# Expert chunks 0 to 5 taken rank by rank, with one chunk prepared ahead, in a fused attention and mixture-of-experts kernel

## What is computed

```python
w, idx = _gate(xf, gate_w)                 # 1024 tokens, the best 6 of 32 experts
c = zeros((T, E)).at[arange(T)[:, None], idx].add(w)
g = einsum('td,eid->tei', xf, w11)         # E = 32, i = 128, d = 256
u = einsum('td,eid->tei', xf, w33)
y = einsum('tei,te,edi->td', silu(g) * u, c, w22)
shared = silu(xf @ sw1.T) * (xf @ sw3.T) @ sw2.T
return y + shared
```

## Time and profile before

| what | value |
|---|---|
| runs | 410.45, 412.38 and 405.9 us, median 410.45 |
| profiled execution, its own time | 408.52 us |
| its span, first to last instruction | 406.7 us |
| mean granted TensorE clock | 0.849 of full speed |
| busy: PE, DVE, POOL, ACT | 287.6, 257.0, 211.5, 167.7 us |

### The profile page before, as it was taken

How to read it: one execution, slowest core, us unless ns; L and a number is a source line. 1 busy time by engine, 2 the same in 40 slices (tenths; PEclk the granted TensorE clock), 3 DMA queues, 4 the chain that set the end, 5 groups by cost and what they waited for, 6 DMA issues and landing times.

```text
span 406.7 us, 5245 instructions
## 1 busy us (share of the span) xinstructions
PE 287.6 (71%) x1471; PEld 216.1 (53%) x1471; DVE 257.0 (63%) x758; ACT 167.7 (41%) x368; POOL 211.5 (52%) x238
## 2 busy tenths in 40 slices
PE   0899975610699999339899396583579899999600
PEld 0444433310679888026466174462569799998400
DVE  4499998570253533175886878798645566656366
ACT  1500003530255554525636534220266688887400
POOL 2577751037433555410511077767775677778830
PEclk9999997655599999958967778789598999999955
DMA  8556699723376651489989222325469855798598
GB/s 236 163 139 180 178 271 270 222 84 116 124 218 196 187 175 50 147 282 319 305 256 365 78 79 92 106 89 178 146 182 289 250 168 156 240 283 274 176 374 283
DMA packets 66062, 80.56 MB, mean 198 GB/s; under 512 B 7643, under 2 KB 55061, under 8 KB 66035
## 3 DMA queue, kind: packets, MB, share of 16 engines
q1 hardware_dynamic: 56547, 62.45, 52.2%
q0 software_dynamic: 7296, 16.93, 12.2%
q10 hardware_dynamic: 2192, 0.86, 0.8%
HBM read 43.70 MB, written 38.01 MB: 201 GB/s over the span
## 4 chain that ended last, share of the span: by engine, by line
PE 52%; DVE 15%; DMA 11%; POOL 10%; issue 7%; ACT 4%; POOLq 1%; SPq 0%; ACTq 0%; DVEq 0%
PE banks L1817 9%; POOL rows_s L688 7%; PE banks L1664 6%; PE banks L1665 5%; PE banks L1666 5%; DMA y_s<-y_sb,place 4%; PE banks L1784 4%; PE banks L1645 4%; PE banks L1646 3%; PE banks L1647 3%; PE banks L1674 2%; POOL y_s L726 2%; DMA rowbuf<-rows_s 2%; PE banks L1910 2%; DMA pre_own<-y_s 2%
## 5 line engine op out<-in xcount | busy, mean ns | idle before, releaser
L726 POOL DMA_INDIRECT y_s<-y_sb,place x88 | 90.8, 1032 | 47.1 <-ACT y_sb L857 24.1
L688 POOL DMA_INDIRECT rows_s<-staged,slot_i x64 | 64.2, 1003 | 57.2 <-DVE staged L1168 38.9
L1664 PE MATMUL banks<-xT_hi,w_hi 128*128 128x224 f32 (+1 forms) x192 | 63.8, 332 | 8.2 <-DVE w_lo L1421 8.0
L1665 PE MATMUL banks<-xT_lo,w_hi 128*128 128x224 f32 (+1 forms) x192 | 56.5, 294 | 0.0
L1666 PE MATMUL banks<-xT_hi,w_lo 128*128 128x224 f32 (+1 forms) x192 | 56.4, 294 | 0.0
L1664 PEld LDWEIGHTS banks<-xT_hi,w_hi 128*128 128x128 f32 x192 | 38.5, 201 | 13.9 <-DVE w_lo L1421 10.9
L1817 PE MATMUL banks<-down_raw,hid 128*104 128x256 f32 (+1 forms) x176 | 44.0, 381 | 1.6 <-DVE hid L1443 1.4
L1784 PE MATMUL banks<-ident,rowbuf 112*128 112x112 f32 (+1 forms) x176 | 25.3, 275 | 27.2 <-DMA rowbuf<-rows_s 22.7
L765 ACT ACTIVATE h_sb<-x_sb,shift,rstd 128x256 f32<-128x256 f32 x22 | 11.7, 590 | 68.8 <-DVE shift L1027 68.8
L857 ACT ACTIVATE y_sb<-banks,meta 112x256 f32<-112x256 f32 (+1 forms) x88 | 36.3, 471 | 8.0 <-PE banks L1817 7.5
L1665 PEld LDWEIGHTS banks<-xT_lo,w_hi 128*128 128x128 f32 x192 | 38.5, 201 | 0.7
(11 more groups left out here) (241 smaller groups left out, 595.5 us busy)
## 6 DMA issues: line engine op xcount, KB each, us to landing
rows_s<-empty SPq DMA_DIRECT2D x5, 2730.0 KB
up_raw<-in_up SPq DMA_DIRECT2D x38, 256.0 KB, 4.7
rowbuf<-rows_s SPq DMA_DIRECT2D x32, 227.5 KB, 3.4
down_raw<-in_down SPq DMA_DIRECT2D x38, 128.0 KB, 4.6
rows_s<-empty SPq DMA_DIRECT2D x7, 633.8 KB
rowbuf<-rows_s SPq DMA_DIRECT2D x8, 316.9 KB
toep<-filt_s SPq DMA_DIRECT2D x16, 128.0 KB, 3.3
h_sb<-y_s SPq DMA_DIRECT2D x4, 512.0 KB, 5.3
```

The lines of the kernel that those rows point to most:

```text
L688: nc.gpsimd.indirect_dma_start(out=rows_s, out_offset=bass.IndirectOffsetOnAxis(ap=slot_i[:, k, b:b + 1], axis=0), in_=staged[:, b, k % BU ...
L726: nc.gpsimd.indirect_dma_start(out=y_s[n], out_offset=bass.IndirectOffsetOnAxis(ap=place[slot][0:TILE[n], t:t + 1], axis=0), in_=y_sb[slot ...
L1664: nc.tensor.matmul(out, wh, xh, start=start, stop=False)
L1665: nc.tensor.matmul(out, wh, xl, start=False, stop=False)
```

## The change

For chunks 0 to 5 each engine prepares only one chunk ahead (`prepares`: steps 0 to 3 prepare s + 1; step 4 prepares 5 and then 6; step 5 prepares 7). From step 6 on the order is that of before. On PE a step of these is `up(s)`, `down(s-1)`, `turn_rows(s+1)`; step 4 is `up(4)`, `down(3)`, `turn_rows(5)`, `down(4)`, `turn_rows(6)`. On ACT it is silu, `take_y(s-1)`, `high_parts(s+1)`. Before the loop only chunk 0 is prepared. PE's wait for all of `add_shared` moves from ahead of chunk 0's transposes to behind `up(0)`. On DVE chunk 0 is split ahead of `stage_values(10)`, and step 0 (with the split of chunk 1) stands between `add_shared(1)` and `stage_values(11)`. `table_turns` moves behind step 8 and `table_codes` behind step 10. On SP the up weights of chunk 5 and the down weights of chunk 4 are loaded ahead of the wait for the last rank, and no longer behind it. For the first feed-forward block nothing changes.

```diff
-        def run_steps(eng, n, step):
+        def run_steps(eng, n, step, begun=0):
             for i in range(FIXED[n]):
-                for r in range(4):
+                for r in range(0 if i else begun, 4):
                     step(i, r, i == 0, False)
...
+        def by_rank(n, i, r):
+            return n == 1 and isinstance(i, int) and 4 * i + r < TOPK1
+
+        def prepares(i, r):
+            return ((1,), (1,), (1,), (1,), (1, 2), (2,))[4 * i + r]
...
-                    if not (last and r >= 2):
+                    if n == 1 and first and r == 3:
+                        sp.wait_ge(f.w_split, 2)
+                        load(up_raw[1][:], of_unit(up_d, TOPK1 - 1, 0), f.up_in[1])
+                        sp.wait_ge(f.down_done, 1)
+                        load(down_raw[0][:], of_unit(down_d, TOPK1 - 2, 0), f.down_in[0])
+                        sp.wait_ge(f.x_split, 2)
+                        wait_sent(TOPK1 - 1)
+                        load(rowbuf[1][0:TILE[n], 0:TILES[n]], rows_of(TOPK1 - 1), f.rows_in[1])
+                    elif not (last and r >= 2):
...
-                    if not first and not own:
+                    if not first and not own and not (n == 1 and isinstance(i, int) and s == TOPK1 - 2):
...
+                    if by_rank(n, i, r):
+                        if 0 < s < TOPK1 - 1:
+                            take_y(i, r, -1)
+                        high_parts(i, r, prepares(i, r)[0])
+                        if s == TOPK1 - 2:
+                            take_y(i, r, 0)
+                            high_parts(i, r, 2)
+                        return
...
+                    if by_rank(n, i, r):
+                        for ahead in prepares(i, r):
+                            low_parts(i, r, ahead)
+                    elif first:
...
+                    if n == 1 and isinstance(i, int) and s == 8:
+                        table_turns(1, 2)
+                    if n == 1 and isinstance(i, int) and s == 10:
+                        table_codes(1)
...
                     stage_values(9)
                     shared_hid(3)
                     add_shared(0)
-                    table_turns(1, 2)
+                    low_parts(0, 0, 0)
                     stage_values(10)
                     add_shared(1)
+                    step(0, 0, True, False)
                     stage_values(11)
-                    table_codes(1)
-                low_parts(0, 0, 0)
-                low_parts(0, 1, 0)
...
-                    pe.wait_ge(x_added, X_ATT1 + 4)
...
+                    if by_rank(n, i, r):
+                        s = 4 * i + r
+                        up(i, r, first)
+                        if 0 < s < TOPK1 - 1:
+                            down(i, r, -1)
+                        if s == 0:
+                            pe.wait_ge(x_added, X_ATT1 + 4)
+                        turn_later(i, r, prepares(i, r)[0])
+                        if s == TOPK1 - 2:
+                            down(i, r, 0)
+                            turn_later(i, r, 2)
+                        return
```

More of the change, by code:

```diff
@@ L322, in ahead_of @@
             def ahead_of(r, prepare):
[L323 to L327, removed]
-            return ahead_of
+                for t in range(2 * r) if r < 2 else (r,):
+                    prepare(t)
+            return ahead_of
+        def by_rank(n, i, r):
+            return n == 1 and isinstance(i, int) and 4 * i + r < TOPK1
+        def prepares(i, r):
+            return ((1,), (1,), (1,), (1,), (1, 2), (2,))[4 * i + r]
         def is_zero(count):
@@ L862, in _ @@
                 high_parts(0, 0, 0)
-                high_parts(0, 1, 0)
+                if n == 0:
+                    high_parts(0, 1, 0)
                 def step(i, r, first, last):
@@ L871, in step @@
                         .then_inc(f.silu_made, 1)
+                    if by_rank(n, i, r):
[6 more added lines that the diff above has]
+                        return
                     if first:
-                        if r and not (n == 0 and r == 2):
+                        if r and r != 2:
                             take_y(i, r, -1)
@@ L1389, in _ @@
                     route_first()
[L1390 to L1399, removed]
-                    table_turns(1, 2)
-                    stage_values(10)
-                    add_shared(1)
-                    stage_values(11)
-                    table_codes(1)
                 def low_parts(i, r, ahead):
@@ L1444, in step @@
                     ins.then_inc(f.hid_made, 1)
-                    if first:
+                    if by_rank(n, i, r):
+                        for ahead in prepares(i, r):
+                            low_parts(i, r, ahead)
+                    elif first:
                         ahead_of(r, lambda t: low_parts(i, t, 2))
@@ L1448, in step @@
                         low_parts(i, r, 2)
-                turns = run_steps(dve, n, step)
+                    if n == 1 and isinstance(i, int) and s == 8:
+                        table_turns(1, 2)
+                    if n == 1 and isinstance(i, int) and s == 10:
+                        table_codes(1)
+                if n == 0:
+                    low_parts(0, 0, 0)
+                    low_parts(0, 1, 0)
+                else:
+                    stage_values(6)
+                    shared_hid(1)
+                    stage_values(7)
+                    stage_values(8)
+                    shared_hid(2)
+                    table_sums(1, 2)
+                    stage_values(9)
+                    shared_hid(3)
+                    add_shared(0)
+                    low_parts(0, 0, 0)
+                    stage_values(10)
+                    add_shared(1)
+                    step(0, 0, True, False)
+                    stage_values(11)
+                turns = run_steps(dve, n, step, n)
                 last_k = TOPK[n] - 1
@@ L1823, in _, with turn_later @@
                 turn_rows(0, 0, 0)
[L1824 to L1828, removed]
+                def turn_later(i, r, ahead=2):
+                    c, first_unit, _, _, _ = chunk_of(n, i, r, ahead)
                     back = (1, 2)[n]
@@ L1831, in turn_later @@
                         pe.wait_ge(f.x_split, c - back + 1)
-                    turn_rows(i, r, 2)
+                    turn_rows(i, r, ahead)
                 def step(i, r, first, last):
+                    if by_rank(n, i, r):
[10 more added lines that the diff above has]
+                        return
                     if first:
-                        if n == 0 and r == 2:
+                        if r == 2:
                             down(i, r, -1)
```

## The result

The changed kernel takes 414.54 us (median of 4 runs, 412.61 to 416.62), the kernel before 410.49 us (4 runs): ratio 1.0137, 95% interval 1.0086 to 1.0188. The medians lie 4.05 us apart and the ratio says 5.6 us, since it compares the means of the fast runs alone and one run of the kernel before (412.38 us) counts as slow. The time is inside the range of the prediction, but the loss is well beyond the 1.4 us that stood there as the likeliest. The profiled execution took 412.66 us with a span of 410.8 us, 4.1 us more than that of the kernel before.

The account below looks back on a forecast made before the run. Bound: the path to `up(9)` at 321.56 us, through chunk 5's late rows and a slow `y_sb` scatter. `up(9)` 0.5 us later plus 0.9 us for the table, on 408.52, gave 409.9 us; range 404.5 to 415.0.

Parts of the forecast that it names:

- the circle of the steps: Steps one chunk ahead: `up(s)`, `down(s-1)`, transposes and split of s + 1, then `up(s+1)`; 5.02 or 7.15 us by clock.
- The rule that what moves `up(9)` moves the end by as much: Landmark: start of `up(9)`, 321.56 us before; its shift moves the end equally unless a later wait takes it back.
- When step 0 starts: Start of the chunks on PE: `up(0)` at about 282.0, `up(1)` at about 288.0, `stage_values(11)` hidden with 4.6 us to spare.
- What a step costs rank by rank: Steps one chunk ahead: 5.02 us at full clock, 7.15 at half, against ranks coming every 5.04 us.
- Which clock?: PE in the new steps, idle about 2.3 us each: clock goes up and down, mean of 6.09 us a step likeliest.
- The sum, to `up(9)`: `up(4)` at 306.3, chunk 5 turned at 309.4, `up(5)` at 312.4, `up(9)` at 322.1: 0.5 us after 321.56.
- slow rival: Clock lost for all of steps 1 to 4: `up(9)` at 326.3, 5.6 us slower, 414.1 us; chance 18%.
- The table in the loop: `table_turns` and `table_codes` on DVE behind steps 8 and 10: 0.9 us lost, bounds 0 and 4.44.
- The stall of 312 to 321: `place` held by a 7.32 us `y_sb` scatter: already in the landmark, does not come back; landed by 318.8.
- The loads that SP issues ahead of the last rank: 384 KB of early weights: cost at nothing; at best take 1.3 us out of what queues later.
- The rule of the Trainium skill: Matmul bursts parted by long DMA waits begin at half rate; by it alone the sum is 414.1 us.
- The first rival: Clock holds: steps of 5.04 us, sends the floor, `up(9)` at 318.3, 3.3 us gained, 406.1 us; chance 27%.

Follow-up runs that it names:

- e5b: Changed kernel with 9, 5 and 10 small matmuls into an unused bank filling PE's gaps, rerun on another chip: 408.17 us, ratio 0.9980 to the kernel before.
- e3: Kernel before with only `table_turns` and `table_codes` moved behind steps 8 and 10: 409.64 us, ratio 0.9999.
- e6b: Changed kernel with PE's gaps filled as in e5b and the table's pieces put back ahead of the loop: 409.12 us, ratio 0.9987 to the kernel before.
- h2b: h1 without the early loads, the weights of chunk 5 behind its rows again: 411.67 us, ratio 1.0020 to the kernel before.
- h1: Kernel before, two chunks ahead, but chunk 5 prepared only in step 4, with the change's early weight loads: 407.45 us, ratio 0.9939.
- e1: Changed kernel with `table_turns` and `table_codes` put back ahead of the loop: 414.17 us, ratio 1.0114 to the kernel before.

## Why the prediction was right or wrong

The step that failed is the clock's share of the steps, with the tail as a smaller second. The view of how the chunks begin and the circle of the steps held. The rule that what moves `up(9)` moves the end by as much did not: `up(31)` lost 1.2 us more than `up(9)` in the changed kernel, and in e5b it gained 1.6 us less. The places, by the prediction's own steps:

- *When step 0 starts.* Foreseen 282.0 and 288.0 for `up(0)` and `up(1)`; 282.76 and 288.70 came, in a trace that is 0.6 us later from ahead of the chunks. `stage_values(11)` was hidden. The last rank started at 295.25 and not at 294.45, which the prediction names as a sign of being wrong, but POOL waited for nothing (0.30 us between scatters, as ever), and the last scatter started at 299.04 for 298.77.
- *What a step costs rank by rank.* At full clock 5.02 was foreseen and 5.15 came; at half clock 7.15 and 7.32. `down` was priced too low: 0.68 us is its time between transposes and an `up`. Between an `up` and transposes, as in these steps, it took 0.86 us at full clock (304.78 to 305.64) and 1.70 at half (291.40 to 293.10), for 1.36 foreseen; the 3.1 us of the rest, 2.92 measured, hid half of that.
- *Which clock?* This step failed. I took the mean, 6.09 us, as the likeliest. Steps 1 and 2 and the `up` of step 4 ran at half clock, and only step 3 at full. Up to `up(4)` the steps average (308.49 - 288.70) / 3 = 6.60 us; chunk 5 was turned at 312.37 for 309.4, and `up(5)` started at 315.23 for 312.4. Of the 2.5 us that `up(9)` came later than foreseen, 1.5 lie in steps 1 to 3 and 0.8 in `up(4)` and `down(3)`.
- *The sum, to `up(9)`.* Foreseen 322.1 (0.5 late), measured 324.63. The slow rival, with 18% on it, said 326.3; it had the mechanism. That its 414.1 us lie so near the measured 414.54 is partly luck: its `up(9)` was 1.7 us too late, since one step kept the clock, and it had nothing for the tail, in which another 1.2 us was lost from `up(9)` to `up(31)` (4.4 - 3.2). The likeliest sum also stood on the profiled execution's 408.52 us, 2 us under the median of the runs, so that 409.9 us was no loss at all against them.
- *The table in the loop.* 0.9 us foreseen; some 0.4 us in the trace of the changed kernel (2.97 - 2.585), nothing that can be measured in the runs (e3 at 0.9999, e6b no better than e5b).
- *The stall of 312 to 321.* It did not come back, as foreseen: `up(6)` to `up(9)` came 2.5 to 2.6 us apart.
- *The loads that SP issues ahead of the last rank.* Cost at nothing, 1.3 us at best. In the changed kernel they delay chunk 5's rows by about 1.2 us, which nobody waits for. Their worth shows only where `down(4)` stands ahead of chunk 6 and PE has caught up with chunk 5: h2b against h1, 0.8%.
- *The rule of the Trainium skill* ("TensorE: Matmul & The Clock Gate", section "HAM oscillation — how this bites in real kernels") says that matmuls parted by waits that are long enough begin each time at the slow clock; taken for every step, that was the slow rival's case. The trace agrees for three of the four steps and not for `up(3)`, and e5b shows that the loss goes when the gaps are filled. I gave it too little weight, against one gap that spoke otherwise.

The two gaps that I had weighed against each other tell less than I took from them. Their 2.20 and 2.10 us are stretches cut inside the gaps; PE's idle times were 2.28 us, which kept the clock, and 2.40 us, which lost it:

```profile
304.72 0.98 PE L1784 MATMUL banks<-ident,rowbuf 112*128 112x112 f32 x4 [2.40 <-DMA rowbuf<-rows_s]
```

The work ahead of them doesn't part them: 6.5 us of matmuls stood ahead of the first, and 11.5 us, broken once for 0.26 us, ahead of the one that lost the clock. Nor do the new steps among themselves: `up(2)` and `up(3)` both follow some 5.4 us of matmuls at 0.50 and a gap of 1.97 and 1.96 us, but the first began at 0.50 and the second at 1.00; the clock rose in its gap (0.84 from 301.4 to 302.0, 1.00 from there on). So these rows can't tell which step gets which clock. That three of the four got the slow one can be seen, here and in e1.

So the likeliest sum was off mainly by one term, the clock's share of the steps, and a loss clear of noise came where I had called it no change.

How much of the 1.4% is the clock? The filled kernels stand at 0.9980 (changed) and 0.9983 (before). At a held clock the change is therefore neutral within 0.5%, and the loss is what the half clock costs it. The first rival had 406.1 us for a clock that holds: filled, the kernel came near its `up(9)` (18.7 us behind the first send for 17.9) and not its time (ratio 0.9980), as the lead was lost again behind it. Shown is that holding the clock removes the loss; that nothing but the clock differs between the changed kernel and e5b rests on the filling touching only an unused bank and PE's own gaps.

## What to carry to other kernels

Preparing one piece less ahead shortens the path to the first result and puts a wait into every step; price the step at both levels of the clock, and if PE idles for 2 us in each, take the slow level as the likeliest, as in three of four steps here. Where a late arrival is the trouble, move only that arrival back in the order, and keep the pipeline two deep around it: h1 did that and gained 0.6% where the whole reordering lost 1.4%. Weights for a piece that now comes earlier on an engine must be asked for earlier too, or, as `down(4)` in h2b by the order of its loads, the first instruction that needs them takes the place of the wait that was removed.

## What I had not expected of the hardware

- The neighbours of a group of matmuls change its price, from its start to the next group's: `down` took 0.68 us between transposes and an `up` and 0.86 between an `up` and transposes (304.78 to 305.64), both at full clock. With the same neighbours the half clock costs the factor two: 1.70 us (291.40 to 293.10). `up`, with `down` behind it, took 1.44 us at full clock (303.34 to 304.78) and 2.70 at half (288.70 to 291.40).
- Unbroken matmuls don't bring the clock back after a fixed time: in the kernel before some 3 us were enough, from 291 and from 304.8; in the changed kernel it stayed at 0.50 for the 5.30 us from 288.70 to 294.00 and through the gap behind them, while after the next 5.2 us, from 296.00 to 301.20, it rose in the gap.
- Loads in flight lengthen the way of a scatter: with 384 KB of weights more asked for 1 to 2 us ahead of the last scatter, the time from its start to the next load was 4.12 us and not 2.94.
